# Causal attention core: value products one step behind the exponential, and the mask of the maximum inside VectorE's reduction

## The reference

```python
x = x + 0.5 * L0_ffn(layernorm(x))         # token shift, relu^2, sigmoid gate
x = x + L0_linear_attention(layernorm(x))  # 16 heads of 16, chunks, k normalised
x = x + 0.5 * L0_ffn(layernorm(x))
x = x + 0.5 * L1_ffn(layernorm(x))         # base product plus the routed low-rank expert
# L1 attention: rotary q and k, 16 heads of 16
scores = einsum('bhqd,bhkd->bhqk', q, k) * scale
scores = where(causal, -inf, scores)
attn = softmax(scores)
x = x + einsum('bhqk,bhkd->bhqd', attn, v) @ Wo.T
x = x + 0.5 * L1_ffn(layernorm(x))
```

## Time and profile before

| | |
|---|---|
| median of 3 runs | 3236.56 us (3227.16 to 3240.71) |
| profiled execution | 3248.06 us |
| its span | 3246.3 us |
| TensorE (PE) busy | 2891.0 us, 89% |
| TensorE weight loads (PEld) busy | 1811.0 us, 56% |
| VectorE (DVE) busy | 1852.1 us, 57% |
| ScalarE (ACT) busy | 1215.9 us, 37% |
| GpSimd (POOL) busy | 746.2 us, 23% |
| mean granted TensorE clock | 0.922 of full speed |

### The profile page before, as it was taken

One profiled execution on the slowest core, in us unless ns is written; L12 is line 12 of the kernel. 1 busy time (PEld: TensorE's weight loads), 2 busy tenths in 40 slices (PEclk: granted clock), 3 DMA queues, 4 the chain that ended last, 5 costly groups with the idle time before them and its releaser, 6 DMA issues.

```text
span 3246.3 us, 47003 instructions
## 1 busy us (share of the span) xinstructions
PE 2891.0 (89%) x16398; PEld 1811.0 (56%) x16398; DVE 1852.1 (57%) x4515; ACT 1215.9 (37%) x2706; POOL 746.2 (23%) x1276
## 2 busy tenths in 40 slices
PE   3885899899999998999999999999999999989987
PEld 2653565456656665556656566466555566555534
DVE  6443656655666556665566556565566655665532
ACT  1321244344334343443334343343434333343341
POOL 1321222222222222223222222222322222221110
PEclk7886899999999999999999999999999989999986
DMA  1024104311232204311333113322134113233101
GB/s 54 1 59 105 21 16 95 94 27 37 55 109 57 58 16 102 106 39 30 63 83 89 36 38 61 110 57 51 26 92 115 30 30 63 70 89 98 44 21 41
DMA packets 137424, 194.06 MB, mean 60 GB/s; under 512 B 49439, under 2 KB 111214, under 8 KB 127854
## 3 DMA queue, kind: packets, MB, share of 16 engines
q1 hardware_dynamic: 137198, 191.07, 23.9%
HBM read 122.34 MB, written 67.63 MB: 59 GB/s over the span
## 4 chain that ended last, share of the span: by engine, by line
PE 65%; DVE 12%; DMA 7%; ACT 4%; issue 3%; SPq 1%; POOL 1%; DVEq 0%; ACTq 0%; POOLq 0%
PE bank L747 9%; PE bank L730 8%; PE bank L766 8%; DMA stk<-k_halves 6%; PE bank L565 4%; PE bank L658 4%; PE bank L505 3%; PE bank L514 3%; PE bank L672 3%; PE bank L545 3%; ACT pexp L1283 3%; PE bank L496 2%; PE bank L659 2%; DVE mxa L1083 2%; PE bank L475 2%
## 5 line engine op out<-in xcount | busy, mean ns | idle before, releaser
L1283 ACT ACTIVATE pexp<-bank 128x512 f32<-128x512 f32 (+3 forms) x1536 | 675.1, 496 | 934.2 <-PE bank L766 748.2
L1083 DVE TENSOR_REDUCE mxa<-bank 128x1 f32<-128x512 f32 (+3 forms) x1024 | 595.3, 587 | 506.9 <-PE bank L733 296.9
L730 PE MATMUL bank<-stk,stq 128*128 128x512 f32 (+3 forms) x1536 | 604.0, 415 | 148.2 <-DVE mxa L1083 53.2
L747 PE MATMUL bank<-stq,stk 128*128 128x512 f32 (+3 forms) x1536 | 592.3, 444 | 73.9 <-ACT pexp L1283 66.5
L730 PEld LDWEIGHTS bank<-stk,stq 128*128 128x128 f32 x1536 | 300.6, 198 | 466.8 <-issue 408.3
L1431 POOL TENSOR_SCALAR_AFFINE_SELECT pexp<-pexp 128x256 f32<-128x256 f32 x512 | 217.1, 428 | 911.5 <-ACT pexp L1283 911.4
L747 PEld LDWEIGHTS bank<-stq,stk 128*128 128x128 f32 x1536 | 281.9, 198 | 253.8 <-ACT pexp L1283 181.5
L766 PE MATMUL bank<-pexp,vsm 128*32 128x512 f32 (+3 forms) x3072 | 345.1, 523 | 0.0
L1083 DVE TENSOR_REDUCE mxb<-bank 128x1 f32<-128x128 f32 (+3 forms) x512 | 248.0, 484 | 167.5 <-PE bank L733 165.2
L733 PE MATMUL bank<-maskneg,identb 128*128 128x128 bf16 x1024 | 243.4, 238 | 0.0
L1349 POOL TENSOR_SCALAR_AFFINE_SELECT arena<-arena 128x512 f32<-128x512 f32 x128 | 78.4, 636 | 438.9 <-ACT arena L1187 438.9
(11 more groups left out here) (185 smaller groups left out, 4146.8 us busy)
## 6 DMA issues: line engine op xcount, KB each, us to landing
stq<-q_halves SPq DMA_DIRECT2D x128, 256.0 KB
arena<-rope_table SPq DMA_DIRECT2D x8, 2048.0 KB
q_halves<-arena SPq DMA_DIRECT2D x32, 512.0 KB, 2.9
k_halves<-arena SPq DMA_DIRECT2D x32, 512.0 KB, 2.8
stk<-k_halves SPq DMA_DIRECT2D x64, 256.0 KB
stk<-k_halves SPq DMA_DIRECT2D x128, 128.0 KB
v_rows<-arena SPq DMA_DIRECT2D x16, 544.0 KB, 4.1
vsm<-v_rows SPq DMA_DIRECT2D x16, 544.0 KB, 3.8
```

What stands on the lines that cost most here:

```text
L730: last = mm(bk[:, 0:k1 - k0], stq[b_][:, h % 2, qb * P:(qb + 1) * P], stk[b_][:, h % 2, k0:k1], start=True, stop=not diag)
L747: mm(ps(j)[:, 0:n], stk[b_][:, j, kb * P:(kb + 1) * P], stq[b_][:, j, (c + 1) * CH - n:(c + 1) * CH], start=True, stop=True).then_inc(s["t ...
L1083: nc.vector.reduce_max(dst, r_bank("s", g, i)[:, 0:k1 - k0], AX).then_inc(s["r_used"], 1)
L1283: nc.scalar.activation(pexp[:, u % NPX, j, 0:n], ps(j)[:, 0:n], ACT.Exp, scale=DK ** -0.5).then_inc(s["exp_done"], 1)
```

## The change

The value products are issued one core step earlier: at even u, for the pair (u - 2, u - 1). The mask product and its identity are removed. For the diagonal units the maximum is taken by `tensor_tensor_reduce`, which adds the mask to the scores, writes the sum back to the PSUM bank and gives the row maximum in a second output; the other units keep `reduce_max`. The mask tile grows to 512 columns (zeros ahead of the last 128), and a buffer `dg` of another stage becomes narrower in its last dimension.

```diff
-        identb = sb("identb", [P, P], BF16)
-        maskneg = sb("maskneg", [P, P], BF16)
+        maskneg = sb("maskneg", [P, CH], BF16)
-        dg = sb("dg", [P, 2, 4, HP])
+        dg = sb("dg", [P, 2, 4, NR + 1])
...
-                    diag = k1 == P * (qb + 1)
-                    last = mm(bk[:, 0:k1 - k0], stq[b_][:, h % 2, qb * P:(qb + 1) * P], stk[b_][:, h % 2, k0:k1],
-                              start=True, stop=not diag)
-                    if diag:
-                        last = mm(bk[:, k1 - k0 - P:k1 - k0], identb[:], maskneg[:], start=False, stop=True)
-                    last.then_inc(s["r_full"], 1)
+                    mm(bk[:, 0:k1 - k0], stq[b_][:, h % 2, qb * P:(qb + 1) * P], stk[b_][:, h % 2, k0:k1],
+                       start=True, stop=True).then_inc(s["r_full"], 1)
...
-                    if part == 1 and u % 2 and 3 <= u < NU * NB + 2:
-                        values(u - 2)
+                    if part == 1 and u % 2 == 0 and 2 <= u < NU * NB + 1:
+                        values(u - 1)
...
-                        nc.vector.reduce_max(dst, r_bank("s", g, i)[:, 0:k1 - k0], AX).then_inc(s["r_used"], 1)
+                        sc = r_bank("s", g, i)[:, 0:k1 - k0]
+                        if k1 == P * (qb + 1):
+                            nc.vector.tensor_tensor_reduce(out=sc, in0=sc, in1=maskneg[:, CH - (k1 - k0):CH], scale=1.0, scalar=LOWEST,
+                                                           op0=ALU.add, op1=ALU.max, accum_out=dst).then_inc(s["r_used"], 1)
+                        else:
+                            nc.vector.reduce_max(dst, sc, AX).then_inc(s["r_used"], 1)
```

More of the change, by code:

```diff
@@ L36 @@
 MASKED = -1e30
+LOWEST = -3e38
 PAD = 8
@@ L221, in _ @@
                 nc.gpsimd.memset(rawd[:], 0.0).then_inc(w_mem, 1)
-                for t, v in ((ident, 0.0), (identb, 0.0), (maskneg, 0.0), (mask01, 1.0), (hmask, 1.0), (ones, 1.0)):
+                for t, v in ((ident, 0.0), (maskneg, 0.0), (mask01, 1.0), (hmask, 1.0), (ones, 1.0)):
                     nc.gpsimd.memset(t[:], v).then_inc(w_pool, 1)
@@ L229, in _ @@
                     nc.gpsimd.memset(first[:, e:e + 1], float(NE - e))
-                pool.wait_ge(w_pool, 6)
+                pool.wait_ge(w_pool, 5)
                 def select(t, op, fill, base, pattern, cm):
@@ L236, in _ @@
                 select(ident[:], ALU.not_equal, 1.0, 0, [[-1, P]], 1).then_inc(w_pool, 1)
-                select(identb[:], ALU.not_equal, 1.0, 0, [[-1, P]], 1).then_inc(w_pool, 1)
-                select(maskneg[:], ALU.is_ge, MASKED, 0, [[-1, P]], 1).then_inc(w_pool, 1)
+                select(maskneg[:, CH - P:CH], ALU.is_ge, MASKED, 0, [[-1, P]], 1).then_inc(w_pool, 1)
                 select(mask01[:], ALU.is_ge, 0.0, 0, [[1, P]], -1).then_inc(w_pool, 1)
                 select(hmask[:], ALU.is_ge, 0.0, 0, [[-DK, H // KT]], 1).then_inc(w_pool, 1)
-                pool.wait_ge(w_pool, 11)
+                pool.wait_ge(w_pool, 9)
                 select(hmask[:], ALU.is_ge, 0.0, DK - 1, [[DK, H // KT]], -1).then_inc(w_pool, 1)
@@ L250, in _ @@
                 pe.wait_ge(w_in, 16 * NLOAD)
-                pe.wait_ge(w_pool, 7)
+                pe.wait_ge(w_pool, 6)
                 for m in range(7):
@@ L318, in _ @@
                 nc.vector.tensor_copy(rsim[0:PROJ, 6], rsim[0:PROJ, 7]).then_inc(w_dve, 1)
-                dve.wait_ge(w_pool, 12)
+                dve.wait_ge(w_pool, 10)
                 nc.vector.reduce_sum(pmask[:], hmask[:].rearrange("p (i a) -> p a i", a=2), AX)
```

## The result

The changed kernel takes 3109.47 us (3102.13 to 3121.12), against 3237.75 us for the kernel before (one run more than in the table ahead of the prediction): ratio 0.9604, 95% interval 0.9577 to 0.9631, so -128 us.

A forecast was written before the change was run, and what follows sets the result against it. TensorE was taken as the bound (89% busy, 65% of the chain): mask products -48, move -60, fused operation +27, given back +24, sum -57 us, so a 3180 us median; forecast's own range 3150 to 3210, 8 in 10 3120 to 3255.

The forecast's parts named there:

- Which line is the bound, and the wait that goes: Attention core on TensorE: ScalarE's exponentials wait 748 us for value products, which was to fall under 150.
- The mask edit: Mask of the maximum moved from TensorE to VectorE: -48 us for the products, +27 for the fused operation.
- the 48: Removing the mask products from TensorE: -48 us, from their 637 pieces on the chain of waits.
- the prediction's lower bound of 24 us: Mask products on TensorE: only -24 us if half stand where TensorE would wait in any case.
- The fused operation: VectorE's fused add and maximum: 0.12 us more each than the plain reduction, together +27 us (0 to 112).
- the prediction's 229 places: Fused operation: 143 reductions on the chain and 86 TensorE waits for a bank, each charged the operation's extra time.
- The move, "I take -60, near the pieces of the chain": Value products one step earlier on TensorE, freeing the exponential's slot sooner: -60 us, between 27 and 118.
- The 98 pieces: Exponentials directly behind value products on the chain, 50.3 us together, named as what the move could remove.
- Given back. A quarter of the 108: +24: Allowance against TensorE's -108 us for places where another path is nearly as late, such as loads of stacks: +24 us.
- more than forecast: Rival, chance 0.20: all mask products count at -68 us and nothing is given back, -111 us, 3126 us.
- the +9 us that the prediction worked out for it: Fused operation's accumulator read as a second VectorE instruction: 0.04 us more at each of 229 places, +9 us.

The follow-up runs named there:

- e2: The changed kernel with the value products back at their old place, so only the mask moves to VectorE: 3216.51 us, ratio 0.9928 to the kernel before.
- e3: The kernel before without any mask of the maximum (no mask product, no fused add), value products at the old place: 3200.26 us, ratio 0.9887.
- e9: The kernel before with each of the 1024 mask products issued twice: 3271.35 us, ratio 1.0087.
- e1: The kernel before with only the value products issued one step earlier, mask product and plain reduction kept: 3135.33 us, ratio 0.9676.
- e7: As e6, with five slots of exponentials in place of four, value products at the old place: 3131.51 us, ratio 0.9674 to the kernel before.
- e6: As e3, with one buffer in place of two for a pass's sum and result, four slots of exponentials: 3199.98 us, ratio 0.9881.
- e11: As e7, with the value products issued one step earlier as well: 3103.44 us, ratio 0.9572 to the kernel before.
- e4: As e3, with the value products issued one step earlier: 3104.69 us, ratio 0.9584 to the kernel before.

## Why the prediction was wrong

*Which line is the bound, and the wait that goes:* right. ScalarE's wait for value products is gone, the scores' wait for it fell to 175 us (150 forecast), L761 waits 8.6 us for the select, under the 20 named, and the score products wait 85.7 us for reductions, as before and under the 130 named.

*The mask edit:* right in its sum, -21 against -23 us (e2), by two errors that cancel, which is luck. The products were worth 37 us (e3; the interval just reaches the 48). Two things go with that. The granted clock fell with the products (below). And they had been cover: without them the next scores wait longer for exponentials, e3 against the 181.5 and 66.5 us before:

```profile
PEld bank L742 <- ACT pexp L1279: 234.9, 525, 1.7
...
PE bank L742 <- ACT pexp L1279: 78.5, 182, 1.1
```

This is what the prediction's lower bound of 24 us was for. How much is the clock's and how much the lost cover's is not shown; in e9, with twice the products, these waits stayed as they were (181.7 and 62.0 us). The fused operation cost 6 to 13 us and not 27. The 0.12 us an operation were three times the 0.041 by which VectorE's busy time grew; the prediction's 229 places at 0.041 would be 9 us.

*The move, "I take -60, near the pieces of the chain":* this is the term that failed, at -105 us (e1). It was taken as one thing and is two.

The first is the slot's wait, which the 60 us were for. It measured 67 us (e7 against e6), so this part was sized nearly right. What is missing in it are the hand-overs: the chain shows 0.60 us of exponential in a pair at the end, and removing it takes 3.94 - 3.16 = 0.78 us off the pair. The 98 pieces hold 50.3 us; times 0.78 / 0.60 they are 65 us. In the last 96 steps lie 28 of the pieces with 13.5 us, by the same factor 17.5 us, and the slot gave 16 us there.

The second is the place of the value products, for which the prediction had no gain at all. It wrote of the even steps that no value product is left as cover and counted this against the move. The place is worth some 28 us instead, with the slot's wait already gone (e11 against e7). About half of them seem to hang on what else shares the step, by the estimate above: in even steps the value products meet the narrow score products, in odd ones the wide. The order list has these widths; I did not look at it. The score products' wait for their banks differs only where the time does; what else is in it stays open. Together 67 and 28 are the 96 us that the move is worth without mask products (e4 against e3); the 105 of e1 are the same within the intervals.

*"Given back. A quarter of the 108: +24":* as a term of the sum nothing came of it. The parts e1 and e2 add up to the whole. What e1's -105 holds of it can't be taken apart: the loads of stacks do wait longer (105.6 us on both sides of L728, 81.8 for L730 before), and the transposes that share the banks of the score products now wait 20.3 us for reductions (L778 and L784), where they waited 2.1 (L783 and L789). An allowance for other paths should have named one with a time.

45 us from the move, 24 from the allowance and 2 from the mask are the 71 us between -57 and -128. Of the rivals, "more than forecast" had the right direction with 0.20, for the wrong reason: it left the move at 60 and counted the mask products in full, at 68 where 37 came.

*What a page said:* the rule of the Trainium skill ("VectorE: DVE Perf Modes", "Two Vector instructions with no wait between them"), that an operation which also writes its accumulator is two instructions, is what the trace shows: 1024 reads of 142 ns. As a reason against the edit it weighed little, since they overlap: the +9 us that the prediction worked out for it would come on top of 27, and the whole operation cost 6 to 13.

## What to carry to other kernels

A buffer that is freed in the same step as, and behind, the work that refills it puts the consumer's time on the path once per round; free it a step earlier, and where nothing else covers it, count the whole round's difference (0.78 us here), not the piece that the chain shows (0.60). Read the last stretch by itself: an eighth of the steps held 30 of 105 us here. That the clock differs there too belongs to such a reading. Before moving work to another step, add up what else is in the step it leaves and in the one it enters.

## What the runs showed of the hardware

TensorE's granted clock moved with each edit of its work. In the profiled executions its mean was 0.922 before, 0.908 and 0.910 without mask products (e2, e3), 0.932 with twice as many (e9), and 0.929 with the move alone (e1). Over all runs the ranges are 0.917 to 0.932 before, 0.906 to 0.920 in e2 and e3, and 0.932 to 0.938 in e9; e1, with 0.924 to 0.937, overlaps the kernel before. In steps 0 to 671 of e2 it is 0.93 in place of 0.95:

```profile
391.00:2937.00 2546.00, 2330.75 (x12965) 1452.91 (x12963) 1577.21 (x4664) 1029.28 (x2306) 625.29 (x1056) 0.93 0.26 63
```

The clock has two levels, 2.4 and 1.2 GHz. By these, a mean of 0.922 over 3246 us is 506 us at the lower one, 0.910 over 3211 is 578, 0.932 over 3270 is 445. So the kernels with fewer products on TensorE spent more time at the lower level, and the one with more products less. The direction fits the 37 us for removing and the 28 us for doubling what the chain held for 48. The size does not follow from it: 72 us more at half the clock could cost up to 36 us, more than the 11 us between 48 and 37, and e3's longer wait for exponentials would come on top. That the clock is the cause was not tried by itself.
